# x1 laid out by sequence and channel group in DRAM, v read back a step later, and the late mixing bias broadcast in two parts

## What is computed

```python
def reference(x, cond_128, fside_S_0, ...):
    # _L0_cond_ref: per sequence a 32 x 32 mixing matrix and a bias, from cond_128
    out = jnp.einsum('boi,bih->boh', agg_w, x) + agg_b[:, :, None]
    # _L0_attn_ref: 32 query heads, 8 key/value heads of 16, rope, causal, over the 32 rows
    attn = jax.nn.softmax(scores, axis=-1)
    out = jnp.einsum('bkgqm,bkmd->bkgqd', attn, v)
    # _L0_cond2_ref: convolution with 9 taps along the 512 values, 4 groups of 8 rows, plus a bias
    out = lax.conv_general_dilated(x, weight, (1,), [(4, 4)], feature_group_count=4)
    # _L0_ffn_ref: base product plus 8 routed low-rank experts
    return base_out + lora
    ...
    x = x + _L0_attn_ref(_L0_cond_ref(x, ...), ...)
    x = x + _L0_ffn_ref(_L0_cond2_ref(x, ...), ...)
```

## Time and profile before

| | |
|---|---|
| median of 3 runs | 653.37 us (650.11 to 654.2) |
| profiled execution, its own time | 651.24 us |
| its span (first to last instruction) | 649.3 us |
| mean granted TensorE clock | 0.988 |
| PE busy | 616.8 us, 95% of the span |
| PE weight loads | 508.9 us, 78% (beside the matmuls) |
| DVE busy | 474.8 us, 73% |
| POOL / ACT busy | 224.6 us / 200.3 us |
| DMA: share of 16 engines' span on SP's queue | 45.6% |
| chain that ended last | PE 88%, DMA 6%, DVE 3% |

### The profile page before, as it was taken

How to read it: one execution, slowest core, us unless ns; L and a number is a source line. 1 busy time by engine, 2 the same in 40 slices (tenths; PEclk the granted TensorE clock), 3 DMA queues, 4 the chain that set the end, 5 groups by cost and what they waited for, 6 DMA issues and landing times.

```text
span 649.3 us, 12985 instructions
## 1 busy us (share of the span) xinstructions
PE 616.8 (95%) x4363; PEld 508.9 (78%) x4363; DVE 474.8 (73%) x1169; ACT 200.3 (31%) x475; POOL 224.6 (35%) x181
## 2 busy tenths in 40 slices
PE   5984999999999999999999999999999999999876
PEld 4663788888888888888888888888888888888654
DVE  3565577788777777787877777787777777887742
ACT  4342232333323323233223323233233323333210
POOL 7353133333333332333333332333333333333310
PEclk9998899999999999999999999999999999999998
DMA  7658334445554344444553334454543434454430
GB/s 173 121 145 238 74 84 94 106 120 118 122 122 105 89 97 96 107 121 118 122 119 100 93 90 95 118 120 120 122 111 90 97 95 101 120 118 106 107 83 32
DMA packets 87509, 71.57 MB, mean 110 GB/s; under 512 B 48342, under 2 KB 70518, under 8 KB 84169
## 3 DMA queue, kind: packets, MB, share of 16 engines
q1 hardware_dynamic: 86016, 70.89, 45.6%
q10 hardware_dynamic: 1336, 0.24, 0.2%
q0 software_dynamic: 144, 0.28, 0.2%
HBM read 51.86 MB, written 19.53 MB: 110 GB/s over the span
## 4 chain that ended last, share of the span: by engine, by line
PE 88%; DMA 6%; DVE 3%; SPq 1%; ACT 1%; issue 1%; DVEq 0%
PE ps L398 34%; PE ps L571 9%; PE ps L565 8%; PE ps L624 6%; PE ps L591 5%; PE ps L583 5%; PE ps L498 4%; PE ps L612 4%; PE ps L535 3%; DMA x_dram<-x1p 3%; DMA scratch<-x_dram 2%; PE ps L599 2%; PE ps L555 2%; PE ps L579 1%; PE ps L538 1%
## 5 line engine op out<-in xcount | busy, mean ns | idle before, releaser
L889 POOL TENSOR_TENSOR qk<-network,t 128x640 f32<-128x640 f32 x31 | 48.3, 1559 | 171.2 <-DVE t L1066 171.2
L398 PE MATMUL ps<-wqkv_hi,y_hi 128*128 128x512 f32 (+1 forms) x256 | 87.3, 341 | 2.3 <-DVE raw L1085 1.5
L398 PE MATMUL ps<-wqkv_hi,y_lo 128*128 128x512 f32 (+1 forms) x256 | 87.1, 340 | 0.0
L398 PE MATMUL ps<-wqkv_lo,y_hi 128*128 128x512 f32 (+1 forms) x256 | 86.9, 340 | 0.0
L901 POOL TENSOR_TENSOR raw<-x1p,basebB 128x512 f32<-128x512 f32 x32 | 49.2, 1538 | 100.9 <-DVE x1p L1140 100.9
L1074 DVE TENSOR_TENSOR qk_t<-ps,cst 128x512 f32<-128x512 f32 x32 | 22.1, 692 | 67.1 <-PE ps L553 67.1
L714 ACT ACTIVATE qk_t<-ps 128x512 f32<-128x512 f32 x32 | 19.1, 598 | 142.5 <-PE ps L555 142.5
L714 ACT ACTIVATE raw<-ps 128x256 f32<-128x256 f32 (+1 forms) x96 | 40.2, 453 | 66.2 <-PE ps L612 64.5
L776 ACT ACTIVATE raw<-raw 128x512 f32<-128x512 f32 x64 | 40.6, 634 | 54.3 <-DVE raw L1085 54.3
L398 PEld LDWEIGHTS ps<-wqkv_hi,y_hi 128*128 128x128 f32 x256 | 48.6, 190 | 10.0 <-DVE raw L1085 2.7
L873 POOL TENSOR_TENSOR raw<-raw,rz 128x512 f32<-128x512 f32 x32 | 33.7, 1052 | 65.1 <-DVE rz L1095 65.1
(11 more groups left out here) (180 smaller groups left out, 1482.7 us busy)
## 6 DMA issues: line engine op xcount, KB each, us to landing
scratch<-x_dram SPq DMA_DIRECT2D x96, 259.8 KB, 4.3
x_dram<-x1p SPq DMA_DIRECT2D x32, 260.0 KB, 4.5
xm<-x SPq DMA_DIRECT2D x32, 256.0 KB, 3.8
xr<-x SPq DMA_DIRECT2D x32, 256.0 KB, 4.0
out<-raw SPq DMA_DIRECT2D x32, 256.0 KB, 2.1
v_dram<-vS SPq DMA_DIRECT2D x32, 64.0 KB
vB<-v_dram SPq DMA_DIRECT2D x128, 16.0 KB, 2.2
mixb<-mixb_dram SPq DMA_DIRECT2D x1, 1792.0 KB, 8.9
```

The source lines that it names most:

```text
L398: last = mm(dst, a, b, start=(n == 0), stop=(n == 3 * len(left) - 1))
L889: nc.gpsimd.tensor_tensor(qk[:, :], t1, t2[:, :], ALU.add).then_inc(qk_sb, 1)
```

## The change

x1_dram becomes [16 (sequence, row group)][32 (row in its group, phase)][130], so the store writes each partition's 520 values as one piece, and the three reads take 16 pieces of 128 values for each destination row. The destination tile has no pads any more. `load_values` is split: the store of v of group t+1 stays in step t but moves behind the output, ahead of x1's store; the read back moves into the next step, behind the three reads of x1. `late_mixing` is gone: the mixing matrices are read at the end of step 0, behind x1's store and the input rows, the biases of groups 4 to 11 (512 KB) at the end of step 1, those of groups 12 to 31 (1280 KB) at the end of step 2. DVE waits for both before `next_y(4)`. In step 32 the last group of three `keep_warm` matmuls, behind the convolution, becomes two.

```diff
-        xcF = scratch[0:SHIFTS * S, 0:NB * PH * (P + 2)]
-        xc = xcF.rearrange("p (q n) -> p q n", n=P + 2)[:, :, 0:P]
+        xc = scratch[0:SHIFTS * S, 0:NB * PH * P].rearrange("p (q n) -> p q n", n=P)
...
-        x1_dram = nc.dram_tensor("x1_dram", [CG * PH, NB * PH, P + 2], F32, kind="Internal").ap()
+        x1_dram = nc.dram_tensor("x1_dram", [NB * PH, CG * PH, P + 2], F32, kind="Internal").ap()
...
-            def late_mixing():
-
-                sp.wait_ge(mixw_out, 16)
-                load_mixw(sp, 4, G, mixw_in)
-                sp.dma_start(mixb[:, 4 * P:], mixb_row[4 * P:].partition_broadcast(P)).then_inc(mixb_in2, 16)
+            def late_bias(lo, hi):
+
+                sp.dma_start(mixb[:, lo * P:hi * P], mixb_row[lo * P:hi * P].partition_broadcast(P)).then_inc(mixb_in2, 16)
...
                     for s in range(SHIFTS):
-                        sp.dma_start(xcF[S * s:S * (s + 1), 0:x1_row],
-                                     x1_dram.rearrange("r q n -> r (q n)")[:, s:s + x1_row]).then_inc(xc_in, 16)
-                if live(t + 1):
-                    load_values(t + 1)
-                if peeled(t, 0):
-                    late_mixing()
+                        sp.dma_start(xc[S * s:S * (s + 1), :, :],
+                                     x1_dram[:, :, s:s + P].rearrange("q r n -> r q n")).then_inc(xc_in, 16)
+                if live(t) and not peeled(t, 0):
+                    load_values(t)
                 if live(t - 2):
                     sp.wait_ge(out_sb, t - 1)
                     sp.dma_start(group(out_g, t - 2), outS).then_inc(out_st, 16)
+                if live(t + 1):
+                    store_values(t + 1)
                 if live(t):
                     sp.wait_ge(x1_sb, t + 1)
-                    sp.dma_start(x1_dram.rearrange("r q n -> q r n"), x1p[:, :, :]).then_inc(x1_out, 16)
+                    sp.dma_start(x1_dram.rearrange("q (i j) n -> (q i) j n", j=PH), x1p[:, :, :]).then_inc(x1_out, 16)
                 if live(t) and live(t + 1):
                     sp.dma_start(xr[:, :], group(x_g, t + 1)).then_inc(xr_in, 16)
+                if peeled(t, 0):
+                    sp.wait_ge(mixw_out, 16)
+                    load_mixw(sp, 4, G, mixw_in)
+                if peeled(t, 1):
+                    late_bias(4, 12)
+                if peeled(t, 2):
+                    late_bias(12, G)
...
                 if peeled(t, G):
-                    keep_warm(3)
+                    keep_warm(2)
...
                 if peeled(t, 3):
-                    dve.wait_ge(mixb_in2, 16)
+                    dve.wait_ge(mixb_in2, 32)
```

More of the change, by code:

```diff
@@ L324, in _ @@
             mixb_row = mixb_dram.rearrange("b s -> (b s)")
-            x1_row = NB * PH * (P + 2) - 2
             sp.wait_ge(y_ps, 1)
@@ L329, in _, with store_values, load_values @@
             sp.dma_start(mixb[:, P:4 * P], mixb_row[P:4 * P].partition_broadcast(P)).then_inc(mixb_in, 16)
-            def load_values(u):
+            def store_values(u):
                 sp.wait_ge(vS_sb, u + 1)
                 sp.dma_start(v_dram.rearrange("(m b) c -> b m c", b=NB), vS[:, :]).then_inc(v_out, 16)
+            def load_values(u):
                 sp.wait_ge(v_out, 16 * (u + 1))
@@ L340, in _ @@
             sp.wait_ge(pads_sb, 1)
+            store_values(0)
             load_values(0)
```

## The result

The changed kernel takes 659.67 us (median of 7 runs, 656.77 to 662.21), the kernel before 653.23 us on the same chip (median of 7, 650.11 to 655.78). The ratio is 1.0096 with a 95% interval of [1.006, 1.0131]: 1% slower. The forecast was 650.5 us with a range of 645 to 657, so both the sign and the range were missed. The profiled execution took 657.08 us (span 655.1) against 651.24 (span 649.3), so the two traces can account for 5.8 us.

What follows compares the result with a forecast made beforehand. PE was taken to bound the loop's 18.35 us periods, leaving gains only at the ends. Terms -5.3 - 1.9 + 6.4 + 2.3 - 3.3 gave -1.8 us, 649.4 to 651.6 us; stated 650.5 us, range 645 to 657.

Steps and rivals of the forecast that it cites:

- g): Tail: first store lands earlier but v comes behind x1, net -0.4; second store's gain and less slow clock; -3.3 us in all.
- a): Step 1: the 8.02 us wait for x1 goes, PE waits 2.7 us for v instead; -5.3 us (-4.3 to -6.3).
- b): Step 1: part of the half-speed stretch after the first wait is won back; -1.9 us (0 to -3.1).
- Bounds, steady period: Loop: PE busy for all 18.35 us of a period, so gains can lie only at the kernel's two ends.
- c): Step 3: new wait for the second broadcast, DVE held 7.2 us and PE 5.4; +6.4 us (+5.2 to +7.5).
- d): Step 3: slower clock after PE's new idle stretch of over 5 us; +2.3 us (0 to +3.1).
- e): Loop's steady periods: v lands later but with 1.9 us in hand before values, so 0.
- f): Step 2: first broadcast stands ahead of x1's and v's reads, but values(2) has 2 to 3 us in hand; 0.
- The second store's part: Tail: the second x1 store has nothing of v behind it, which removes the 1.75 us wait; -1.7 us.
- Rival 2: Whole kernel: the new wait costs more than the old one; +5.3 us, 656 us, up to 657.5; chance 0.15.
- Rival 3: Whole kernel: short waits leave the clock alone and transfers are quick; -8.9 us, 642.3 to 644.5 us; chance 0.19.
- The signs of being wrong: Profile after: prediction wrong if loop periods are longer, the broadcast lands before 97, or the clock stays full throughout.

Runs made afterwards that it cites:

- e10: Changed kernel with v stored and read back in one go as before, ahead of the output and x1's store; 651.0 us, ratio 0.9989 to the kernel before.
- e11: e10 with matrices and both broadcasts behind x1's reads of steps 1, 2 and 3, the second broadcast awaited only in the loop; 637.99 us, ratio 0.9788.
- e7: Changed kernel with unread matmuls filling PE's waits in step 1, step 3 and step 31; 652.27 us, ratio 0.9993 to the kernel before.
- e2: Changed kernel with x1_dram's old layout, store and reads, queue order kept as changed; 676.96 us, ratio 1.0387 to the kernel before.
- e5: e3 with matrices and both broadcasts behind x1's reads of steps 1 to 3, the second awaited only in the loop; 641.85 us, ratio 0.986.
- e3: Changed kernel with v's reads put back ahead of x1's three reads; 651.4 us, ratio 1.0019 to the kernel before.
- e9: e4 with x1 rows 768 B apart and unshifted reads, so pieces start at multiples of 256 B (partly wrong inputs); 648.74 us, one execution.
- e4: Kernel before with only x1_dram's layout, its store, its reads and xc changed; 648.08 us, ratio 0.9954.

## Why the prediction was wrong where it was

The step that failed is the tail's, g), by 5.0 us: the wait that the moved v adds there was given no clock cost. The second is step 1, a) and b), by 2.8 us.

- **Bounds, steady period: right.** 18.35 us, and the ends decide. Where the time lies was read rightly; its sign was not.
- **a) The first wait.** Right that it goes from x1 to v; 4.82 us instead of 2.7. From the start of x1 of group 0, v was to land 12.0 us later and landed 14.2 later. The step that failed is "I reckon 1 us" for what stands ahead of v, and a quick issue of x1's three reads: the issue took 2.80 us instead of 1.2 to 1.8, the landing 4.02 instead of 3.2. The store's landing (2.3 taken, 2.05 to 2.1 measured) was right. e10 and e11 show the cause, which the prediction had noted as "448 KB of matrices in short pieces" and not priced: without them ahead, step 1 is 6.0 us shorter (22.45 to 16.43).
- **b) The clock.** -1.9 was too much: the 4.82 us brought the half clock as the 8.02 had. The slow stretch (59.55 to about 63.8, 4.2 us) costs 2.1 us instead of 3.1, so b) is near -1.0. Together with a), -4.39 instead of -7.2.
- **c), d) Step 3: the mechanism right, the sum partly by luck.** +8.44 against +8.7. The waits were 1 us longer than forecast, DVE's 8.18 (7.2) and PE's 6.40 (5.4): the broadcast took 7.86 us to land, not 6.4, though it was issued 2.0 us after the start of that step's x1, where 2.4 were reckoned. By the estimate from the Trainium skill that stood beside it, 5.0 us for it, the term would have been further off. The routing that was to cost 0.9 us on top kept PE waiting 0.50 in e7, at full clock, and not at all in the changed kernel, where the slow stretch hides it. From x1 of group 2 to the first queries it is 6.6 us more than before, and from there to x1 of group 3 1.9 more, of which e7 has 0.6 at full clock. So c) came to about +7.2 instead of +6.4 (whose own parts add up to 6.3), d) to +1.3 instead of +2.3, and the two misses hold each other.
- **e) Steady periods.** The sum (0) held, its reason didn't: 1.9 us in hand were forecast, 0.7 are there in the period shown and 0.1 at the least. The last read of v was issued 0.8 us earlier than reckoned; the failed term is its landing, priced at 2.1 us as in a free queue, 4.09 measured. It waits for x1's reads ahead of it, and their short pieces are less than half of that: over the loop it lands in 2.1 us with nothing ahead (e10), 3.3 behind three reads in rows of 8.3 KB (e2) and 4.2 behind the 1536 short pieces. e2 shows how little room was left: 2.3 us more at the store cost 15 us.
- **f) Step 2.** "2 to 3 us in hand" were not: v's last read landed 0.67 us late (3.93 us after issue), +0.72.
- **g) Tail: the largest miss,** -3.3 forecast, +1.7 measured. The second store's part came: -2.7 behind x1 of group 31, the wait 0.21 instead of 1.75. The loss is the first part. v of group 31 was priced at 1.1 us of delay, which idle time behind it would swallow; it waited 1.78 us, and idle time did swallow most (the waits of before for the routing and x1, 0.31 and 0.96 us, are gone). But the wait came close behind another of 1.64 us, which every kernel here has and which alone left the clock full, and PE then ran 9.4 us at 1.2 GHz: 4.5 us by e7. The step that failed is that the clock was priced for step 1, step 3 and the second store, and not for the wait that the moved v adds here, though the earlier trace rows had 1.75 us with a slower convolution behind it.
- **Rivals.** Rival 2 came nearest (the upper ends of c and d, the lower of a, b and g), with a chance of 0.15. Its price was added up wrongly: +5.3 on the median of 653.37 is 658.7 us, not 657.5, and so it lay above the stated range of 645 to 657. The measured median lies 1.0 us above that again, since the tail wasn't in it with a loss. Rival 3 (short waits leave the clock alone) is refuted by the 4.82 and 1.78 us waits and by e7.
- **The signs of being wrong.** None of the three came: the periods kept their length, the broadcast landed at 97.95, and the clock fell. The tail, where the largest miss lay, had no sign of its own.

The misses in a, e, f and the wait in g share one step: v's landing was priced as in a queue with little or nothing ahead of it.

## What to carry to other kernels

The landing time of a small transfer is that of what stands ahead of it in its queue: when a transfer is moved, price it by its new neighbours (pieces as well as bytes), not by its own median from the old place. Put large transfers that are needed a period later behind the small ones of the period and wait for them in the period of their first use; a split that puts a large part right ahead of its own waiter only moves the wait. A wait of TensorE costs twice, itself and the slow stretch behind it, and even two waits of under 2 us in a row brought it: in the tail 1.78 us of waiting, itself hidden for the most part, brought 4.5 us of slow matmuls.

## What the runs showed of the hardware that I had not expected

- **Issuing became slow where many short pieces were queued.** A read of x1 that takes 0.33 to 0.49 us to issue took 1.79 behind the matrices and 2.90 behind the second broadcast and two other reads of x1; the input tile 2.16 in e10; the four matrix transfers 5.86 in e11 behind the reads of x1, 2.4 to 2.6 where the queue was emptier. In e2, where the reads of x1 are long rows, their issue behind the same broadcasts stayed at 1.3 to 1.4 us for all three together. The prediction had issue times in its terms, but those of an emptier queue; that they grow by 1 to 3 us was in none of them.
- **The clock after the same wait differs between executions.** PE waits 1.50 to 1.54 us for the softmax ahead of the first queries in every kernel. In the execution of before it stays at full speed:

```profile
34.17 0.51 PE L398 MATMUL ps<-wqkv_hi,y_hi 128*128 128x512 f32 x1 [1.50 <-DVE raw L1085]
34.52 0.39 PE L398 MATMUL ps<-wqkv_lo,y_hi 128*128 128x512 f32 x1
```

In that of e11 it is at half speed:

```profile
33.73 0.80 PE L405 MATMUL ps<-wqkv_hi,y_hi 128*128 128x512 f32 x1 [1.50 <-DVE raw L1092]
34.33 0.63 PE L405 MATMUL ps<-wqkv_lo,y_hi 128*128 128x512 f32 x1
```

Such stretches go with the start of x1 of group 0: 45.3 to 47.1 us where none lies ahead of it, 48.7 with 6.8 us of half clock (e11), 51.0 with about 13.7 us (e5, e7). It is one reason why that start varies, and why medians, not one profile, decide about 1%. The Trainium skill (TensorE: Matmul & The Clock Gate, Why this matters for your kernels) warns of long gaps; these rows show the clock down at one of 1.50 us in one execution and not in another. In the tail a wait of 1.64 us alone left the clock full in before and e3; with 1.78 us more behind it, it fell.

- **A store in whole rows landed in half the time:** x1's 260 KB in 128 pieces of 2080 B take 2.1 us, in 512 pieces of 520 B 4.5. The number of pieces is not all of it, since in e9 512 such pieces, put at multiples of 256 B, take 3.2. The reads in pieces of 512 B, by contrast, lost only 0.6 (e4) to 0.9 us (after) against rows of 8.3 KB.
